# Layer 0 attention in a deeper pipeline, the read-out first, with one extra fp32 product in front of each three transposes

## The chip, the cores and the metric

The program runs on 1 core of one Trainium2 chip. The metric is the device time of one execution in microseconds (us), lower is better. A core has five engines that run side by side and wait for each other by semaphores: TensorE (PE: products and transposes, results into PSUM), VectorE (DVE), ScalarE (ACT), GpSimd (POOL) and SyncE (SP, which issues DMAs here).

## The reference, cut to what matters

The whole network is one layer of neighbourhood attention on 4 images of 56x56 pixels (layer 0), one layer of full attention over 3136 tokens, and a routed feed-forward layer. The change touches only layer 0's attention: each pixel looks at a 7x7 window, with 8 heads, a low rank of 4 for queries and keys, and values of 32 numbers.

```python
attn = jnp.einsum('bhijc,bhikjlc->bhijkl', q, k_win)
attn = attn + bias.transpose(0, 1, 3, 2, 4)[None]
attn = jax.nn.softmax(attn.reshape(B, nh, H, W, K * K), axis=-1)
attn = attn.reshape(B, nh, H, W, K, K)
out = jnp.einsum('bhijkl,bhikjld->bhijd', attn, v_win)
```

## The kernel before, in words

`layer0_attend` handles 8 iterations (`it`: 2 groups of 4 heads, times 4 images). Each iteration has 28 blocks (`n`: 4 row blocks by 7 column blocks) of 112 pixels, so there are 224 blocks. For each block and each of 4 heads (`hh`; `m = 4 n + hh` counts the heads' tiles) the work is:

1. PE `scores` (L452): 112 queries against 280 keys, four products side by side, one PSUM bank a head.
2. DVE `maxima` (L509): add the bias (which masks what is outside a window), write `sm`, keep the row's extreme in `mx`.
3. ACT `exponentials` (L559): exponential into the tile `P`, with the row's sum in `rs`.
4. DVE `normalise` (L516, L519): reciprocals for a pair of heads, then two multiplications of `P`.
5. PE `turn` (L462): three transposes of `P` into one of three PSUM banks.
6. ACT `copy_turned` (L567): that bank into `PTs`.
7. PE `mix` (L474): 12 products of `PTs` with the values into the single bank OUT. An fp32 product is recorded as two instructions, a transpose or an fp32r product as one, so the trace counts 24 here.
8. DVE `read_out` (L527): bank OUT into `yT`, from where SP stores it.

POOL's `place` (L425 and L428) rearranges the next iteration's queries and keys, a pair of casts for each of four pieces; the piece `rb` waits until 28 (rb + 1) tiles of the present iteration are scored. SP loads values (L359) a row block ahead and the next queries and keys (L350, L352).

The order of the work is written out by hand, engine by engine. Before, PE does scores of block n, turns block n-1 and mixes block n-2. DVE does the maxima of n, normalises the first pair of n, reads out n-2, normalises the second pair. ACT does four exponentials of n, then four copies of n. Each engine runs iterations in hardware loops (`Fori`) whose body is one iteration of 28 blocks.

Of the kernel before, what the change touches and what calls it, by code (L numbers as in the profile page):

```python
# [281 lines left out]
def layer0_attend(nc, A, S):  # L282
# [6 lines left out]
    with ExitStack() as ctx:  # L289
# [22 lines left out]
        P = sb("P", [TT, 8, KEYS])  # L312
# [13 lines left out]
        steps = sem("steps")  # L326

        def since(eng, semaphore, it, each, k):

            if not isinstance(it, int) or it * each + k > 0:  # L330
                eng.wait_ge(semaphore, it * each + k)
# [12 lines left out]
        def _(sp):  # L344
# [23 lines left out]
            def store(g, b, it, rb):  # L368
                sp.wait_ge(out_read, it * NBLK + 7 * (rb + 1))
                sp.sem_inc(steps, 1)  # L370
                since(sp, stored, it, 4 * 16, 16 * rb)
                if not isinstance(it, int):
                    sp.sem_inc(steps, 1)
# [3 lines left out]
            def body(g, b, before, after, switch=False, switched=False):  # L377
                it = g * B + b
                for rb in range(ROW_BLOCKS):
                    since(sp, mixed, it, NBLK, 7 * rb)  # L380
                    if not isinstance(it, int):
                        sp.sem_inc(steps, 1)
                    if rb < ROW_BLOCKS - 1:
                        load_values(g, b, rb + 1)
                    elif after is not None:
                        load_values(after[0], after[1], 0)
                    if rb > 0:
                        store(g, b, it, rb - 1)
                    elif before is not None:
                        store(*before, it - 1, ROW_BLOCKS - 1)  # L390
                    if rb == 0 and after is not None:
                        sp.wait_ge(placed, it * 8 + 8)
                        if not isinstance(it, int):
                            sp.sem_inc(steps, 1)
                        load_qk(*after)
                    if switch and rb == 1:
                        load_bias(1, 0)
                    if switch and rb == 3:
                        load_bias(1, 1)
                    if switched and rb == 0:  # L400
                        load_bias(1, 2)
# [8 lines left out]
            body(0, 0, None, (0, 1))  # L410
            with sp.Fori(1, B - 1) as b:
                body(0, b, (0, b - 1), (0, b + 1))
            body(0, B - 1, (0, B - 2), (1, 0), switch=True)
            body(1, 0, (0, B - 1), (1, 1), switched=True)
            with sp.Fori(1, B - 1) as b:
                body(1, b, (1, b - 1), (1, b + 1))
            body(1, B - 1, (1, B - 2), None)
# [4 lines left out]
        def _(pool):  # L422
# [13 lines left out]
            with pool.Fori(1, ITS) as it:  # L436
                pool.wait_ge(loaded, (it + 1) * NLOAD)
                for rb in range(ROW_BLOCKS):
                    pool.wait_ge(scored, it * U - U + 28 * (rb + 1))
                    pool.sem_inc(steps, 1)  # L440
                    place(it, rb)

        @block.tensor
        def _(pe):
# [11 lines left out]
            def turn(it, n):  # L456
                for hh in range(4):
                    m = 4 * n + hh
                    pe.wait_ge(normed, it * U + m + 1)
                    since(pe, copied, it, U, bank_free_at(m) + 1)  # L460
                    for c, k0 in enumerate(CHUNK_FROM):
                        last = pe.transpose(PS[0:CHUNK, turn_bank(m), TT * c:TT * c + TT], P[:, m % 8, k0:k0 + CHUNK],  # L462
                                            idn[:, :])
                    last.then_inc(turned, 1)
# [13 lines left out]
            def body(it, first):  # L478
                for n in range(NBLK):
                    scores(it, n)  # L480
                    if n >= 1:
                        turn(it, n - 1)
                    elif not first:
                        turn(it - 1, NBLK - 1)
                    if n >= 2:
                        mix(it, n - 2)
                    elif not first:
                        mix(it - 1, NBLK - 2 + n)
# [3 lines left out]
            body(0, True)  # L492
            with pe.Fori(1, ITS) as it:
                body(it, False)
# [5 lines left out]
        def _(dve):  # L500
            def maxima(it, n):
                rb, tc = divmod(n, COL_BLOCKS)
                case = 3 * ROW_CASE[rb] + COL_CASE[tc]
                for hh in range(4):
# [3 lines left out]
                    dve.sem_inc(steps, 1)  # L508
# [4 lines left out]
            def normalise(it, n, pair):  # L513
# [4 lines left out]
                for k in (m, m + 1):  # L518
                    dve.tensor_scalar(P[:, k % 8, :], P[:, k % 8, :], rc[:, k % 8:k % 8 + 1], None, ALU.mult)\  # L519
                       .then_inc(normed, 1)  # L520
# [9 lines left out]
            def body(it, first, fresh):  # L530
                for n in range(NBLK):
                    if fresh and n in (0, 7, 21):
                        dve.wait_ge(bias_loaded[(0, 7, 21).index(n)], (it // B + 1) * 64)
                    maxima(it, n)
                    normalise(it, n, 0)
                    if n >= 2:
                        read_out(it, n - 2)
                    elif not first:
                        read_out(it - 1, NBLK - 2 + n)
                    normalise(it, n, 1)  # L540

            dve.memset(vt[0:14, :, :, 2, :], 0.0).then_inc(zeroed, 1)
            body(0, True, True)
            with dve.Fori(1, B) as it:
                body(it, False, False)
            body(B, False, True)
            with dve.Fori(B + 1, ITS) as it:
                body(it, False, False)
            read_out(ITS - 1, NBLK - 2)
            read_out(ITS - 1, NBLK - 1)  # L550

        @block.scalar
        def _(act):
            def exponentials(it, n):
                for hh in range(4):
                    m = 4 * n + hh
                    act.wait_ge(maxed, it * U + m + 1)
                    since(act, turned, it, U, m - 7)
                    act.activation(P[:, m % 8, :], sm[:, hh, :], ACT.Exp, bias=mx[:, m % 8:m % 8 + 1], scale=-1.0,  # L559
                                   accum_out=rs[:, m % 8:m % 8 + 1]).then_inc(exped, 1)  # L560

            def copy_turned(it, n):
                since(act, mixed, it, NBLK, n - 1)
                for hh in range(4):
                    m = 4 * n + hh
                    act.wait_ge(turned, it * U + m + 1)
                    act.activation(PTs[:, m % 8, :], PS[0:CHUNK, turn_bank(m), 0:3 * TT], ACT.Copy).then_inc(copied, 1)  # L567

            def body(it):
# [4 lines left out]
            body(0)  # L574
            with act.Fori(1, ITS) as it:
                body(it)
# [1585 lines left out]
```

## Time and profile before

| what | us |
|---|---|
| median of 3 runs (lowest to highest) | 8198.59 (8192.75 to 8208.01) |
| profiled execution | 8213.32 |
| its span in the trace | 8211.5 |
| layer 0 attention in it, first score product to last read-out | 1107.9, from 489.4 to 1597.3 |

The profile cuts the span into 40 slices of 205 us. Layer 0 attention is the slices from the third to the eighth. "PEclk" is the clock that TensorE was granted, as a share of 2.4 GHz; 0.50 is 1.2 GHz. In timelines a row is a run of like instructions: start, time until the last one's end, engine, line, operation, tiles, count, and in brackets how long the engine had been idle and what released it. Durations of PE are modelled; the distance from start to start is the better measure, and in one row it is (the row's time minus one instruction's own) over (count - 1).

### The profile page before, as it was taken

The page shows a single profiled execution, that of the slowest core. Times are in us where ns is not written, and L with a number is a line of the kernel's source. Part 1 is how long each engine was busy: PE and PEld are TensorE (multiplying, and loading weights), DVE is VectorE, ACT ScalarE, POOL GpSimd, SP SyncE. Part 2 cuts the span into 40 slices and gives each one's busy share as a digit, 9 for nine tenths or more (in the row PEclk, how much of TensorE's full clock was granted, in tenths as well). Part 3 has the DMA queues.
Part 4 walks back from the last instruction along what each step waited for, and adds up shares of the span by engine and source line. Part 5 has one row for each costly group of instructions (what it writes and reads, how often), then busy time and mean ns, then how long its engine had stood idle before and what let it go on. Part 6 is the DMA issues. An engine that isn't in the chain of part 4 may idle for free. (4 is left out here: it accounts for less than half of the span.)

```text
span 8211.5 us, 152999 instructions
## 1 busy us (share of the span) xinstructions
PE 7229.3 (88%) x45616; PEld 4362.4 (53%) x45616; DVE 5407.6 (66%) x12877; ACT 4102.7 (50%) x9367; POOL 3716.6 (45%) x2395
## 2 busy tenths in 40 slices
PE   4558878798999999999999999999999988809999
PEld 3336555565545545545545555455455333708888
DVE  3347777665987767767767777677677201718888
ACT  0047777622005656555656655556565665104444
POOL 4010001011006666666666656566666666355554
PEclk8755565699559999999999999999999999859999
DMA  5432221277100121121121211201210101711221
GB/s 161 133 104 59 61 65 50 73 253 232 39 13 22 37 55 33 27 58 35 32 61 26 50 43 30 64 22 38 55 38 25 40 4 38 224 29 56 58 57 32
DMA packets 403203, 520.46 MB, mean 63 GB/s; under 512 B 64096, under 2 KB 355474, under 8 KB 399063
## 3 DMA queue, kind: packets, MB, share of 16 engines
q1 hardware_dynamic: 379687, 469.02, 21.2%
q0 software_dynamic: 22640, 40.75, 1.8%
q8 instruction: 429, 7.03, 0.4%
q14 instruction: 447, 3.66, 0.2%
HBM read 339.07 MB, written 200.10 MB: 66 GB/s over the span
## 5 line engine op out<-in xcount | busy, mean ns | idle before, releaser
L1253 DVE TENSOR_REDUCE a_tops<-a_ps 128x1 f32<-128x448 f32 (+1 forms) x5600 | 3074.4, 616 | 1089.0 <-PE a_ps L1155 1071.2
L1376 POOL TENSOR_TENSOR a_added<-a_P 128x896 f32<-128x896 f32 x1344 | 2801.6, 2105 | 2091.9 <-ACT a_P L1353 2091.9
L1353 ACT ACTIVATE a_P<-a_ps 128x448 f32<-128x448 f32 (+1 forms) x5600 | 2657.6, 547 | 2119.0 <-PE a_ps L1224 2087.8
L1224 PE MATMUL a_ps<-a_qp,a_kp 98*128 98x448 f32 (+1 forms) x5600 | 2157.0, 400 | 97.8 <-ACT a_P L1353 72.7
L1155 PE MATMUL a_ps<-a_hk,a_hq 96*128 96x448 f32 (+1 forms) x4900 | 1818.8, 381 | 1.8 <-DMA a_hq<-scratch_q 1.7
L1224 PEld LDWEIGHTS a_ps<-a_qp,a_kp 98*128 98x128 f32 (+1 forms) x5600 | 1031.0, 188 | 1291.4 <-ACT a_P L1353 737.3
L1175 PE MATMUL a_ps<-a_P,a_vt 128*32 128x448 f32 (+1 forms) x11200 | 1336.2, 549 | 0.0
L1155 PEld LDWEIGHTS a_ps<-a_hk,a_hq 96*128 96x128 f32 (+1 forms) x4900 | 916.7, 187 | 263.3 <-DVE a_tops L1253 170.7
L462 PE MATMUL n_ps<-n_idn,n_P 112*98 112x112 f32 x2688 | 517.3, 365 | 194.2 <-DVE n_P L519 177.8
L1191 PE MATMUL a_ps<-a_added,a_ones 128*32 128x448 f32 x5376 | 649.2, 555 | 0.0
L1175 PEld LDWEIGHTS a_ps<-a_P,a_vt 128*32 128x32 f32 (+1 forms) x11200 | 290.1, 109 | 514.1 <-issue 387.9
L462 PEld LDWEIGHTS n_ps<-n_idn,n_P 112*98 112x98 f32 x2688 | 406.1, 180 | 293.3 <-DVE n_P L519 271.6
L567 ACT ACTIVATE n_PTs<-n_ps 98x336 f32<-98x336 f32 x896 | 393.5, 451 | 239.3 <-PE n_ps L462 198.0
L1276 DVE RECIPROCAL a_sums<-a_sums 128x112 f32<-128x112 f32 x224 | 185.4, 836 | 488.8 <-ACT a_sums L1328 488.8
L559 ACT ACTIVATE n_P<-n_sm,n_mx 112x280 f32<-112x280 f32 x896 | 459.5, 518 | 61.4 <-DVE n_mx L509 46.9
L425 POOL CAST n_qp<-n_qn 128x784 fp32r<-128x784 f32 x32 | 52.9, 1655 | 907.6 <-PE n_ps L452 527.4
L1143 PE MATMUL a_ps<-a_kp,a_qp 96*128 96x448 f32 (+1 forms) x700 | 370.2, 726 | 22.5 <-DMA a_kp<-scratch_k 22.5
L509 DVE CUSTOM_DVE_ANT_0 n_sm<-n_ps,n_bias 112x280 f32<-112x280 f32 x896 | 348.3, 445 | 63.4 <-PE n_ps L452 48.1
L519 DVE TENSOR_SCALAR n_P<-n_P,n_rc 112x280 f32<-112x280 f32 x896 | 350.4, 433 | 15.7
L1956 ACT ACTIVATE e_h<-e_ps,e_b 128x512 f32<-128x512 f32 (+1 forms) x256 | 172.1, 672 | 351.4 <-PE e_ps L1916 326.3
L1929 PE MATMUL e_ps<-e_w2h,e_hTh 128*128 128x256 f32 (+1 forms) x1024 | 299.0, 292 | 36.8 <-DVE e_widest L2038 36.8
L1143 PEld LDWEIGHTS a_ps<-a_kp,a_qp 96*128 96x128 f32 (+1 forms) x700 | 198.4, 284 | 194.3 <-DVE a_tops L1253 169.1
(193 smaller groups left out, 7533.6 us busy)
## 6 DMA issues: line engine op xcount, KB each, us to landing
a_qp<-scratch_q SPq DMA_DIRECT2D x168, 224.0 KB, 3.9
a_kp<-scratch_k SPq DMA_DIRECT2D x96, 320.0 KB, 5.4
a_hk<-scratch_k SPq DMA_DIRECT2D x84, 336.0 KB, 5.0
scratch_t<-o_ts SPq DMA_DIRECT2D x56, 448.0 KB, 5.7
scratch_vw<-scratch_v SPq DMA_DIRECT2D x56, 392.0 KB
n_vt<-scratch_vw SPq DMA_DIRECT2D x64, 343.0 KB
a_hq<-scratch_q SPq DMA_DIRECT2D x84, 200.0 KB, 3.2
e_w<-in_w SPq DMA_DIRECT2D x16, 1024.0 KB, 7.0
```

The source lines that it names most:

```text
L462: last = pe.transpose(PS[0:CHUNK, turn_bank(m), TT * c:TT * c + TT], P[:, m % 8, k0:k0 + CHUNK], idn[:, :])
L519: dve.tensor_scalar(P[:, k % 8, :], P[:, k % 8, :], rc[:, k % 8:k % 8 + 1], None, ALU.mult)\
L559: act.activation(P[:, m % 8, :], sm[:, hh, :], ACT.Exp, bias=mx[:, m % 8:m % 8 + 1], scale=-1.0, accum_out=rs[:, m % 8:m % 8 + 1]).then_in ...
L567: act.activation(PTs[:, m % 8, :], PS[0:CHUNK, turn_bank(m), 0:3 * TT], ACT.Copy).then_inc(copied, 1)
L1143: pe.matmul(PS[0:rows_of(t), i % FIRST_BANKS, 0:GW], qp[0:96, hh, 128 * t:128 * t + rows_of(t)], kp[0:96, hh, GW * k:GW * k + GW], start=T ...
L1155: pe.matmul(PS[0:rows_of(t), MAX + i % MAXES, 0:GW], hq[:, 128 * t:128 * t + rows_of(t)], hk[:, GW * k:GW * k + GW], start=True, stop=True ...
L1175: last = pe.matmul(PS[HD * hh:HD * hh + HD, MIX, 0:GW], vt[0:rows, t, HD * hh:HD * hh + HD], P[0:rows, (2 * n + hh // 2) % (2 * RING), hh ...
L1191: last = pe.matmul(PS[HD * hh:HD * hh + HD, SUM, 0:GW], ones[:, :], added2[:, (2 * (PAIRS * j + u) + hh // 2) % 6, hh % 2, :], start=(u == ...
L1224: pe.matmul(PS[0:rows_of(t), i_s % 3, 0:GW], kp[0:98, hh, 128 * t:128 * t + rows_of(t)], qp[0:98, hh, GW * j:GW * j + GW], start=True, sto ...
L1253: dve.tensor_reduce(tops[0:rows_of(t), KT * hh + t, k:k + 1], PS[0:rows_of(t), bank, 0:GW], AX_X, ALU.max).then_inc(topped, 1)
L1353: act.activation(P[0:rows_of(t), (2 * n + pair) % (2 * RING), hh % 2, :], PS[0:rows_of(t), (4 * n + hh) % 3, 0:GW], ACT.Exp).then_inc(expe ...
L1376: pool.tensor_tensor(added2[:, a % 6, :, :], P[:, (2 * n + pair) % (2 * RING), :, :], P[:, (2 * n + 2 + pair) % (2 * RING), :, :], ALU.add ...
```

## The change

All of it is in `layer0_attend`.

- Deep order. PE does scores of n, turns n-2 (was n-1), mixes n-3 (was n-2). DVE reads out n-4 first (was n-2, in the middle), then does the maxima of n, then normalises both pairs of n-1 (was n). ACT alternates one exponential of n with one copy of n-2 (was four and four, copies of n). `P` has 16 slots for it (`RP`, was 8).
- One extra product. In front of the three transposes of each head, PE multiplies the 112x112 unit matrix with itself in fp32 into columns 384 to 495 of the bank that the transposes write. Nothing reads it. It waits for the bank to be free; the wait for `normed` now stands behind it.
- The hardware loops are gone: all eight iterations are written out on every engine, and the waits are on constants.

```diff
-        P = sb("P", [TT, 8, KEYS])
+        RP = 16
+        P = sb("P", [TT, RP, KEYS])
...
             def turn(it, n):
                 for hh in range(4):
                     m = 4 * n + hh
+                    since(pe, copied, it, U, bank_free_at(m) + 1)
+                    pe.matmul(PS[0:TT, turn_bank(m), 384:384 + TT], idn[:, :], idn[:, :], start=True, stop=True)
                     pe.wait_ge(normed, it * U + m + 1)
-                    since(pe, copied, it, U, bank_free_at(m) + 1)
...
                     scores(it, n)
-                    if n >= 1:
-                        turn(it, n - 1)
+                    if n >= 2:
+                        turn(it, n - 2)
                     elif not first:
-                        turn(it - 1, NBLK - 1)
-                    if n >= 2:
-                        mix(it, n - 2)
+                        turn(it - 1, NBLK - 2 + n)
+                    if n >= 3:
+                        mix(it, n - 3)
...
-            body(0, True)
-            with pe.Fori(1, ITS) as it:
-                body(it, False)
+            for it in range(ITS):
+                body(it, it == 0)
...
+                    if n >= 4:
+                        read_out(it, n - 4)
+                    elif not first:
+                        read_out(it - 1, NBLK - 4 + n)
                     maxima(it, n)
-                    normalise(it, n, 0)
-                    if n >= 2:
-                        read_out(it, n - 2)
+                    if n >= 1:
+                        normalise(it, n - 1, 0)
...
+            def body(it, first):
                 for n in range(NBLK):
-                    exponentials(it, n)
-                    copy_turned(it, n)
+                    for hh in range(4):
+                        exponential(it, 4 * n + hh)
+                        if n >= 2:
+                            copy_turned(it, 4 * n - 8 + hh)
```

PE within a steady block, before: the last transposes of a block, its `mix`, the next scores, the next transposes (L462 transposes, L474 mix, L452 scores; `waits` names the semaphores).

```order
L462 MATMUL n_ps<-n_idn,n_P 98x112 [waits n0_copied,n0_normed]
L462 MATMUL n_ps<-n_idn,n_P 98x112 x2
L474 MATMUL n_ps<-n_PTs,n_vt 32x112 [waits n0_out_read,n0_copied]
L474 MATMUL n_ps<-n_PTs,n_vt 32x112 x11
L452 MATMUL n_ps<-n_kp,n_qp 112x280 [waits n0_maxed]
L452 MATMUL n_ps<-n_kp,n_qp 112x280 x3
L462 MATMUL n_ps<-n_idn,n_P 98x112 [waits n0_copied,n0_normed]
L462 MATMUL n_ps<-n_idn,n_P 98x112 x2
```

PE at the same place now (L448 the extra product, L451 transposes, L463 mix, L440 scores).

```order
L448 MATMUL n_ps<-n_idn 112x112 [waits n0_copied]
L451 MATMUL n_ps<-n_idn,n_P 98x112 [waits n0_normed]
L451 MATMUL n_ps<-n_idn,n_P 98x112 x2
L463 MATMUL n_ps<-n_PTs,n_vt 32x112 [waits n0_out_read,n0_copied]
L463 MATMUL n_ps<-n_PTs,n_vt 32x112 x11
L440 MATMUL n_ps<-n_kp,n_qp 112x280 [waits n0_maxed]
L440 MATMUL n_ps<-n_kp,n_qp 112x280 x3
L448 MATMUL n_ps<-n_idn 112x112 [waits n0_copied]
```

A product that waits for the copies alone now stands in front of each group of transposes, and the groups behind the scores are those of two blocks ago.

ACT before, around one block's end (L559 exponential, L567 copy; the register instructions belong to the loop).

```order
L559 ACTIVATE n_P,n_rs<-n_sm,n_mx 112x280 [waits n0_turned,n0_maxed]
L331 REGISTER_ALU
L567 ACTIVATE n_PTs<-n_ps 98x336 [waits n0_turned,n0_mixed]
L567 ACTIVATE n_PTs<-n_ps 98x336 [waits n0_turned] x3
L557 REGISTER_ALU
```

ACT now (L550 exponential, L557 copy).

```order
L557 ACTIVATE n_PTs<-n_ps 98x336 [waits n0_turned]
L550 ACTIVATE n_P,n_rs<-n_sm,n_mx 112x280 [waits n0_turned,n0_maxed]
L557 ACTIVATE n_PTs<-n_ps 98x336 [waits n0_turned,n0_mixed]
L550 ACTIVATE n_P,n_rs<-n_sm,n_mx 112x280 [waits n0_turned,n0_maxed]
L557 ACTIVATE n_PTs<-n_ps 98x336 [waits n0_turned]
```

Exponentials and copies alternate, and no register instruction stands between them.

## Rows read from the trace of the kernel before

**Rows 1.** The page: the span, and the granted clock in 40 slices.

```profile
span 8211.5 us, 152999 instructions
PEclk8755565699559999999999999999999999859999
```

**Rows 2.** Windows view, whole layer 0 attention.

```profile
core 0: us, PE busy (x) PEld busy (x) DVE busy (x) ACT busy (x) POOL busy (x), PEclk, DMA share, GB/s
489.40:1597.30 1107.90, 888.47 (x8960) 658.78 (x8960) 795.71 (x3360) 850.81 (x2688) 94.67 (x58) 0.60 0.23 58
```

**Rows 3.** Waits in that stage: waiter, releaser, total us, times, longest.

```profile
DVE n_rc L516 <- ACT n_P L559: 275.3, 224, 6.9
ACT n_PTs L567 <- PE n_ps L462: 198.0, 328, 5.2
```

**Rows 4.** Timeline of a block at granted clock 0.50.

```profile
1401.99 1.35 PE L474 MATMUL n_ps<-n_PTs,n_vt 98*32 98x112 f32 x24
1403.27 0.58 PE L452 MATMUL n_ps<-n_kp,n_qp 16*112 16x280 f32 x4
1404.22 2.48 PE L462 MATMUL n_ps<-n_idn,n_P 112*98 112x112 f32 x12 [0.38 <-DVE n_P L519]
1407.90 0.58 PE L452 MATMUL n_ps<-n_kp,n_qp 16*112 16x280 f32 x4
```

**Rows 5.** Timeline, PE in a block at granted clock 1.00.

```profile
1202.48 0.43 PE L452 MATMUL n_ps<-n_kp,n_qp 16*112 16x280 f32 x4
1203.43 0.78 PE L462 MATMUL n_ps<-n_idn,n_P 112*98 112x112 f32 x6 [0.52 <-DVE n_P L519]
...
1205.16 0.78 PE L474 MATMUL n_ps<-n_PTs,n_vt 98*32 98x112 f32 x24
...
1206.20 0.40 PE L452 MATMUL n_ps<-n_kp,n_qp 16*112 16x280 f32 x4 [0.26 <-DVE n_mx L509]
```

**Rows 6.** Timeline, DVE and ACT in the same stretch.

```profile
1204.95 0.45 DVE L509 CUSTOM_DVE_ANT_0 n_sm<-n_ps,n_bias 112x280 f32<-112x280 f32 x1
1204.98 0.79 ACT L567 ACTIVATE n_PTs<-n_ps 98x336 f32<-98x336 f32 x2 [0.16 <-PE n_ps L462]
...
1205.32 0.45 DVE L509 CUSTOM_DVE_ANT_0 n_sm<-n_ps,n_bias 112x280 f32<-112x280 f32 x1
...
1206.68 0.52 ACT L559 ACTIVATE n_P<-n_sm,n_mx 112x280 f32<-112x280 f32 x1
1206.82 0.17 DVE L516 RECIPROCAL n_rc<-n_rs 112x2 f32<-112x2 f32 x1 [0.67 <-ACT n_P L559]
...
1207.19 0.52 ACT L559 ACTIVATE n_P<-n_sm,n_mx 112x280 f32<-112x280 f32 x1
...
1208.59 0.45 DVE L509 CUSTOM_DVE_ANT_0 n_sm<-n_ps,n_bias 112x280 f32<-112x280 f32 x1
```

**Rows 7.** The page's groups: ACT's copies.

```profile
L567 ACT ACTIVATE n_PTs<-n_ps 98x336 f32<-98x336 f32 x896 | 393.5, 451 | 239.3 <-PE n_ps L462 198.0
```

**Rows 8.** Timeline at a turn of the hardware loop.

```profile
1184.00 0.58 PE L452 MATMUL n_ps<-n_kp,n_qp 16*112 16x280 f32 x4 [2.65 <-issue]
...
1187.07 2.29 PE L462 MATMUL n_ps<-n_idn,n_P 112*98 112x112 f32 x11 [2.14 <-issue]
...
1192.37 0.53 ACT L559 ACTIVATE n_P<-n_sm,n_mx 112x280 f32<-112x280 f32 x1 [2.52 <-issue]
```

**Rows 9.** Timeline at a pair of POOL's casts.

```profile
1248.32 1.77 POOL L425 CAST n_qp<-n_qn 128x784 fp32r<-128x784 f32 x1 [8.93 <-PE n_ps L452]
...
1249.03 2.85 DVE L519 TENSOR_SCALAR n_P<-n_P,n_rc 112x280 f32<-112x280 f32 x2
...
1250.05 1.67 POOL L428 CAST n_kp<-n_kn 128x784 fp32r<-128x784 f32 x1
```

**Rows 10.** Windows view: three of layer 0 attention, one of layer 1, one of the feed-forward.

```profile
1523.40:1557.60 34.20, 31.59 (x312) 24.09 (x309) 24.11 (x113) 28.60 (x89) 0.00 (x0) 0.50 0.17 43
1202.60:1209.40 6.80, 4.71 (x66) 3.24 (x70) 5.78 (x27) 6.01 (x22) 0.00 (x0) 1.00 0.50 109
1209.40:1219.70 10.30, 9.33 (x104) 7.11 (x96) 7.29 (x36) 8.71 (x29) 0.00 (x0) 0.50 0.28 51
...
2040.00:2450.00 410.00, 381.96 (x737) 203.55 (x741) 373.86 (x705) 6.99 (x15) 11.89 (x4) 0.50 0.15 33
7610.00:7670.00 60.00, 57.68 (x373) 52.16 (x372) 53.99 (x148) 28.44 (x49) 34.47 (x42) 1.00 0.11 33
```

More of the change, by code:

```diff
@@ L325, in layer0_attend @@
         mixed, out_read, stored = sem("mixed"), sem("out_read"), sem("stored")
-        steps = sem("steps")
         def since(eng, semaphore, it, each, k):
-            if not isinstance(it, int) or it * each + k > 0:
+            if it * each + k > 0:
                 eng.wait_ge(semaphore, it * each + k)
@@ L435, in _ @@
                 place(0, rb)
-            with pool.Fori(1, ITS) as it:
+            for it in range(1, ITS):
                 pool.wait_ge(loaded, (it + 1) * NLOAD)
@@ L540, in body @@
-                    normalise(it, n, 1)
-            dve.memset(vt[0:14, :, :, 2, :], 0.0).then_inc(zeroed, 1)
[L543 to L550, printed above, removed]
+                        normalise(it - 1, NBLK - 1, 0)
+                    if n >= 1:
+                        normalise(it, n - 1, 1)
+                    elif not first:
+                        normalise(it - 1, NBLK - 1, 1)
@@ L552, in _ @@
+            dve.memset(vt[0:14, :, :, 2, :], 0.0).then_inc(zeroed, 1)
+            for it in range(ITS):
+                body(it, it == 0, it % B == 0)
+            for pair in range(2):
+                normalise(ITS - 1, NBLK - 1, pair)
+            for n in range(NBLK - 4, NBLK):
+                read_out(ITS - 1, n)
         @block.scalar
         def _(act):
[L554 to L560, printed above, removed]
@@ L575, in _, with exponential, copy_turned @@
-            with act.Fori(1, ITS) as it:
-                body(it)
+            def exponential(it, m):
+                act.wait_ge(maxed, it * U + m + 1)
+                since(act, turned, it, U, m - RP + 1)
+                act.activation(P[:, m % RP, :], sm[:, m % 4, :], ACT.Exp, bias=mx[:, m % 8:m % 8 + 1], scale=-1.0,
+                               accum_out=rs[:, m % 8:m % 8 + 1]).then_inc(exped, 1)
+            def copy_turned(it, m):
+                if m % 4 == 0:
+                    since(act, mixed, it, NBLK, m // 4 - 1)
+                act.wait_ge(turned, it * U + m + 1)
+                act.activation(PTs[:, m % 8, :], PS[0:CHUNK, turn_bank(m), 0:3 * TT], ACT.Copy).then_inc(copied, 1)
@@ new lines, in body @@
+            def body(it, first):
+                for n in range(NBLK):
+                    for hh in range(4):
+                        exponential(it, 4 * n + hh)
+                        if n >= 2:
+                            copy_turned(it, 4 * n - 8 + hh)
+                        elif not first:
+                            copy_turned(it - 1, U + 4 * n - 8 + hh)
+            for it in range(ITS):
+                body(it, it == 0)
+            for m in range(U - 8, U):
+                copy_turned(ITS - 1, m)
```

48 lines of the change are left out of this document (14 added, 34 removed).

## The prediction

> **What bounds the kernel now.** I read first the page's row of the granted clock [rows 1]: in layer 0 attention it stands near half, while the slices of the later layers are mostly at 9. The windows view of the stage [rows 2] gives its size, 1107.9 us for 224 blocks or 4.95 us a block, and a mean clock of 0.60: with only the levels 0.50 and 1.00, a fifth of the time at 2.4 GHz, four fifths at 1.2. No engine is full: PE is busy 888 us of 1108, ACT 851, DVE 796.
>
> The waits [rows 3] show a ring: DVE waits 275 us for exponentials and ACT 198 us for transposes, each in every block. The timeline shows how it closes. At 1.2 GHz a block repeats after 1407.90 - 1403.27 = 4.63 us [rows 4]; at 2.4 GHz after 1206.20 - 1202.48 = 3.72 us [rows 5]. PE's pace sets the block although PE waits in it, because an exponential, its normalisation, its transposes and its copy follow one another with only one block of distance. On top come the turns of the loop, where engines stand in "issue" for 2 to 3 us, PE twice and ACT once [rows 8], and POOL's cast pairs, during which two multiplications of DVE take 2.85 us in place of 0.64 [rows 9].
>
> **The change part by part.**
>
> *The ring goes.* Every consumer now takes what was made a block earlier. What is late next is the sum of work of an engine, so I add these up per block.
> ACT: exponentials start 1207.19 - 1206.68 = 0.51 apart; two copies in a row take 0.79, one is 0.45 [rows 6, 7], so they start 0.34 apart. 4 x 0.51 + 4 x 0.34 = 3.40 us.
> DVE: a maximum every 1205.32 - 1204.95 = 0.37; from the first reciprocal to the next block's first maximum, which holds both normalisations and the read-out, 1208.59 - 1206.82 = 1.77 [rows 6]. 4 x 0.37 + 1.77 = 3.25 us.
> PE at 2.4 GHz: 12 transposes at (0.78 - 0.27)/5 = 0.10, 24 mix instructions about 0.70, scores about 0.25, the turnover to mix 0.1 [rows 5] (0.27, one transpose's own time, is my estimate): 2.25 us.
>
> *The extra products.* One fp32 product is two instructions. They are not in the trace; the nearest row is the transpose with the same 112 columns, 0.10 at 2.4 GHz and (2.48 - 0.39)/11 = 0.19 at 1.2 [rows 4, 5] (0.39 an estimate likewise). 8 a block: 0.8 or 1.5 us. Bounds: 0 (they run while PE waits for `normed`) to twice that, were both the load and the stream of each exposed. I take once. Nothing waits for them but PE's own queue: the transposes behind them, then copies. PE at 2.4 GHz: 3.05 us, below ACT's 3.40. PE at 1.2 GHz: mix up to the next scores 1403.27 - 1401.99 = 1.28, transposes 12 x 0.19 = 2.28, products 1.52, scores about 0.35, turnover 0.13: 5.56 us. So at the low clock PE alone would bound a block, at 5.55 us, 0.9 more than now; at the high one ACT does, and the products are free.
>
> *Which clock.* Before, PE rises to 2.4 GHz after dense stretches at 1.2 and falls again when, at 2.4, it starts to wait: 6.8 us with PE busy 4.71 at 1.00, then 10.3 us with 9.33 at 0.50 [rows 10]. After the change PE at 1.2 GHz never waits, denser than any stretch of this stage before. At 2.4 GHz it works 3.05 of 3.5 us; before it worked 2.25 of 3.72. The feed-forward holds 1.00 over 60 us with PE busy 57.7 [rows 10]. I take it that 2.4 GHz mostly holds, and is lost where PE has to stand still.
>
> *The fast block.* Floor 3.40 (ACT), ceiling 3.72, what the old order reaches at 2.4 GHz. One chain comes close to the floor: read-out 0.27, maximum 0.45, exponential 0.51, copy 0.45, product and transposes 0.6, mix 0.78, with some 0.3 of signals 3.3 to 3.4 us, because bank OUT is single. Two engines and this chain are within 0.15 us; jitter adds up. I take 3.6: 224 x 3.6 = 806 us.
>
> *POOL's casts.* 28 pairs fall into the running stage. Each now held DVE for 2.85 - 0.64 = 2.2 us [rows 9]. DVE has nearly no spare time to catch up; the bounds are 0.5 (slack in `P` and `sm`) and 3.4 (the pair's full length, as all four multiplications now stand in a row). I take 2.0: 56 us.
> By the Trainium skill (SBUF — State Buffer, section on who interferes with whom) VectorE in a two-port mode and GpSimd take a shared port pair by an exclusive lock, and the loser blocks for the whole instruction. The trace agrees: the two multiplications end with the second cast. By that rule alone, which leaves no slack, the term would be the full pairs, 28 x 3.4 = 95 us.
>
> *Clock lost behind these.* If each pair drops the clock for as long as a fast stretch lasts now, 6.8 us, at 5.55 in place of 3.6 per block, it costs 6.8 x (1 - 3.6/5.55) = 2.4 us; 28 x 2.4 = 67 us. Bounds 0 and, for 10.3 us each, 101.
>
> *The loops.* The three waits at a turn, one after the other on the ring, are 2.65 + 2.14 + 2.52 = 7.3 us [rows 8], 7 times: 51 us, which are in the 1108 and not in the new sum. Straight code is new for seven of eight iterations; its fetching costs nothing where no branch is taken [rows 4], bounds 0 and the same 51. Fill and drain of the deeper order: 15 us.
> SP's queries and keys for the next iteration (32 DMAs) need some 35 us of an iteration that is now about 105 long, and values a row block of 25: hidden. The loss if not would be single microseconds per iteration.
>
> *Sum.* 806 + 56 + 67 + 15 = 944 us against 1108: 164 us less. 8213 - 164 = 8049 for an execution like the profiled one; this was 14.7 us above the median of the runs, so 8034, I say 8035. With all terms low (3.45 a block, 28 x 1, 28 x 0.7, 15): 836, 272 less, 7927. With all high (3.72, 95, 101, 20): 1049, 59 less, 8140; with the fetching's 51 as well 8190.
>
> **The rivals.**
>
> *B: the clock goes on swinging.* For it: before, every fast stretch of this stage fell, and PE still has pauses at 2.4 GHz. Against it: PE's waits shrink from 1.5 us to 0.5 a block. With as much time low as high, 6.8 us each: 1.23 + 1.89 blocks in 13.6 us, 4.36 a block, 977 + 56 + 15 = 1048, 60 less, 8139. With 10.3 low to 6.8 high as in [rows 10]: 4.57 a block, 1094, 14 less, 8184, which is no change.
>
> *C, the other side: the clock never rises.* Mechanism: the extra products lengthen PE's block at 1.2 GHz to 5.56 us, PE is the bound, and DVE and ACT have 2 us spare, in which the casts hide. 224 x 5.55 + 15 = 1258: 150 more, 8348. The end at which it costs begins where 3.6 + 1.95 x + 0.25 for the casts reaches (1108 - 15)/224 = 4.88, that is with more than x = 0.53 of the blocks low. For it: 34 us of this stage at PE busy 31.6 stayed at 0.50, and layer 1 has 410 us with 382 busy at 0.50 [rows 10]. Against it: that busy time is modelled and contains waits; the real starts of this stage, with 0.4 and 0.6 us of pause a block, often sufficed to rise.
> The Trainium skill (TensorE: Matmul & The Clock Gate, Part 4) says that transposes do not count as PE-busy in the way products do. If so the products are what counts, and half of PE's time does not: that speaks for C. The trace speaks against: the clock rose in this stage with transposes as its largest part.
>
> *D: a wait of the new order that I don't see* keeps the block at the old pace: nothing but the loops is won or lost, within 16 us of before.
>
> **How the numbers follow.** My forecast 0.54, B 0.31, C 0.10, D 0.05. About 16 us (0.2%) is what a measurement tells from no change. Faster: 0.54 + 0.31 less a tenth of B that ends at no change (0.03) = 0.82, and a third of D, 0.02, gives 0.84. Same: 0.03 + 0.02 = 0.05. Slower: C and the rest of D, 0.11. The range: from all terms low, 7930, up into B, 8165, which leaves out C and the slow end of B. The forecast's own range is 7930 to 8140, the fetching's bound aside, which I hold for unlikely.
>
> **What would show it.** Right: the stage's mean clock above 0.85; starts of ACT's exponentials 0.85 to 0.9 apart, alternating with copies, in 3.45 to 3.7 us a block; ACT busy over 85% of the stage; no "issue" waits of 2 us at iteration ends; DVE's multiplications still stretched at POOL's casts, and a low stretch behind them. Wrong: clock between 0.6 and 0.8 and blocks of two kinds, 3.6 and 5.5 (B); clock 0.50 and 5.5 throughout (C); a block over 3.9 at 2.4 GHz would mean that the chain through bank OUT is longer than I added up.

## The result, and the profile after

The changed kernel takes 7928.72 us (median of four runs, 7921.81 to 7931.02). The kernel before, run beside it, takes 8202.67 us (four runs, 8192.75 to 8208.01). The ratio is 0.9666, its 95% interval 0.9649 to 0.9683. That is 274 us less where 164 were forecast, and the median lies 1 us below the range, whose low end was 7930 (two of the four runs lie inside). The profiled execution took 7931.02 us, against 8213 before.

The page after, beside [rows 1]:

```profile
span 7929.2 us, 152182 instructions
PEclk8779999995599999999999999999999999859999
```

The 5s of layer 0 attention are gone and the stage is about one slice of 200 us shorter. The windows view of the stage, beside [rows 2]:

```profile
490.10:1331.20 841.10, 795.70 (x10752) 634.66 (x10752) 767.28 (x3360) 772.95 (x2688) 93.83 (x58) 0.96 0.29 75
```

The stage went from 1107.9 to 841.1 us, 267 less, which is the change. The other 15 us between the two spans lie behind the stage (6614 us before, 6598 after), in a part that no edit touches and that takes between 6592 and 6623 us in the profiles of the runs below. PE has 1792 more instructions and is still busy for less time, since the granted clock went from 0.60 to 0.96. ACT is now busy 92% of the stage and DVE 91%. Per block the stage takes 3.75 us in place of 4.95.

The waits of the stage after, beside [rows 3] (waiter, releaser, total us, times, longest):

```profile
ACT n_P L550 <- DVE n_mx L498: 108.3, 46, 46.1
PEld n_ps L448 <- ACT n_PTs L557: 98.9, 346, 2.9
...
PE n_ps L451 <- DVE n_P L508: 10.2, 15, 2.6
ACT n_PTs L557 <- PE n_ps L451: 2.0, 4, 1.0
```

Both halves of the old ring are gone. DVE's 275 us for exponentials don't appear, and ACT's 198 us for transposes are 2.0. PE now waits most for free banks, that is for ACT's copies. (46 us of ACT's first row lie ahead of the first block.)

The page's group of the copies after, beside [rows 7]:

```profile
L557 ACT ACTIVATE n_PTs<-n_ps 98x336 f32<-98x336 f32 x896 | 391.1, 437 | 2.6 <-PE n_ps L451 2.0
```

The copies cost ACT what they cost before. What vanished is the idle time in front of them, 239 us before and 2.6 now.

A steady block, timeline, beside [rows 5] and [rows 6]:

```profile
1262.10 0.40 PE L440 MATMUL n_ps<-n_kp,n_qp 16*112 16x280 f32 x4
1262.24 0.27 DVE L516 COPY n_yT<-n_ps 128x112 f32<-128x112 f32 x1
1262.26 0.52 ACT L550 ACTIVATE n_P<-n_sm,n_mx 112x280 f32<-112x280 f32 x1
1262.43 0.45 PE L448 MATMUL n_ps<-n_idn 112*112 112x112 f32 x2
1262.64 0.45 DVE L498 CUSTOM_DVE_ANT_0 n_sm<-n_ps,n_bias 112x280 f32<-112x280 f32 x1
...
1262.77 0.44 ACT L557 ACTIVATE n_PTs<-n_ps 98x336 f32<-98x336 f32 x1
1263.13 0.53 ACT L550 ACTIVATE n_P<-n_sm,n_mx 112x280 f32<-112x280 f32 x1
...
1264.80 0.78 PE L463 MATMUL n_ps<-n_PTs,n_vt 98*32 98x112 f32 x24
1265.52 0.40 PE L440 MATMUL n_ps<-n_kp,n_qp 16*112 16x280 f32 x4
```

The block repeats after 1265.52 - 1262.10 = 3.42 us. Of the 223 distances between two blocks' scores, 202 lie wholly at full clock; their median is 3.417, and 182 of all lie within 0.05 of it. Exponentials and copies alternate on ACT without a gap: 1262.26, 1262.77, 1263.13. PE's longest wait in this block is 0.23 us, for a copy.

The rest is at POOL's casts. In six of seven iterations the first pair (due after 7 scored blocks) comes late: it waits for its DMA until about the 14th block, where the second pair is due too, and both run back to back (once 1 us apart). Timeline there:

```profile
643.04 1.64 POOL L414 CAST n_qp<-n_qn 128x784 fp32r<-128x784 f32 x1 [50.06 <-DMA n_kn<-scratch_qk]
643.23 2.94 DVE L508 TENSOR_SCALAR n_P<-n_P,n_rc 112x280 f32<-112x280 f32 x2
...
644.61 1.39 POOL L417 CAST n_kp<-n_kn 128x616 fp32r<-128x616 f32 x1
...
645.94 1.67 POOL L414 CAST n_qp<-n_qn 128x784 fp32r<-128x784 f32 x1
...
646.27 3.12 DVE L508 TENSOR_SCALAR n_P<-n_P,n_rc 112x280 f32<-112x280 f32 x2
...
647.56 1.67 POOL L417 CAST n_kp<-n_kn 128x784 fp32r<-128x784 f32 x1
...
649.97 0.53 ACT L550 ACTIVATE n_P<-n_sm,n_mx 112x280 f32<-112x280 f32 x1 [4.44 <-DVE n_mx L498]
```

Four casts in a row hold DVE's multiplications for 2.94 and 3.12 us, ACT starves for 4.44 us, and PE with it. The windows of that stretch, of the one behind it, and of the next:

```profile
643.00:650.00 7.00, 3.87 (x49) 2.77 (x48) 6.93 (x12) 2.56 (x10) 6.19 (x4) 1.00 0.28 88
650.40:657.20 6.80, 6.22 (x50) 5.35 (x51) 5.30 (x25) 5.55 (x21) 0.00 (x0) 0.50 0.00 0
657.40:672.00 14.60, 14.59 (x220) 11.48 (x218) 12.72 (x60) 13.65 (x49) 0.00 (x0) 1.00 0.38 98
```

PE works 3.87 of 7.00 us, the clock falls to 1.2 GHz for 6.8 us, and is back at 2.4 behind that. There are ten such low stretches behind the fill, 61 us in all: five behind two pairs in a row, four behind the fourth pair, one behind the first pair of the first iteration, which comes alone. The third pair (21st block) costs a block 0.8 us and leaves the clock as it is. The fourth, due at the last block's scores, costs more:

```profile
1012.40 2.25 POOL L417 CAST n_kp<-n_kn 128x1120 fp32r<-128x1120 f32 x1
1012.49 2.60 DVE L508 TENSOR_SCALAR n_P<-n_P,n_rc 112x280 f32<-112x280 f32 x2
```

Its second cast is the longest, 2.25 us, and the first block of the next iteration takes 5.1 to 6.2 us. By the distances between blocks, seven iterations lose 40 us around the first two pairs (35 of them where these run in a row), 6 at the third and 18 at the fourth, the slow blocks at the low clock included.

### The profile page after: what moved, and what is told of

Read it like the earlier page. It is cut to its first block and busy times, and to the rows that moved or that the text cites. A ratio compares the mean times of both kernels' runs of the same rounds, so it can differ in the third digit from the quotient of the medians.

```text
span 7929.2 us, 152182 instructions
## 1 busy us (share of the span) xinstructions
PE 7120.8 (90%) x47408; PEld 4323.5 (55%) x47408; DVE 5376.1 (68%) x12877; ACT 4022.7 (51%) x9367; POOL 3714.0 (47%) x2395
## 5 line engine op out<-in xcount | busy, mean ns | idle before, releaser
L550 ACT ACTIVATE n_P<-n_sm,n_mx 112x280 f32<-112x280 f32 x896 | 467.9, 522 | 108.4 <-DVE n_mx L498 108.3
L451 PE MATMUL n_ps<-n_idn,n_P 112*98 112x112 f32 x2688 | 421.2, 267 | 10.2 <-DVE n_P L508 10.2
L448 PE MATMUL n_ps<-n_idn 112*112 112x112 f32 x1792 | 373.1, 291 | 30.7 <-ACT n_PTs L557 29.8
L557 ACT ACTIVATE n_PTs<-n_ps 98x336 f32<-98x336 f32 x896 | 391.1, 437 | 2.6 <-PE n_ps L451 2.0
L508 DVE TENSOR_SCALAR n_P<-n_P,n_rc 112x280 f32<-112x280 f32 x896 | 334.2, 415 | 16.0
L448 PEld LDWEIGHTS n_ps<-n_idn 112*112 112x112 f32 x1792 | 255.4, 183 | 112.5 <-ACT n_PTs L557 98.9
```

What stands on the lines that cost most here:

```text
L448: pe.matmul(PS[0:TT, turn_bank(m), 384:384 + TT], idn[:, :], idn[:, :], start=True, stop=True)
L550: act.activation(P[:, m % RP, :], sm[:, m % 4, :], ACT.Exp, bias=mx[:, m % 8:m % 8 + 1], scale=-1.0, accum_out=rs[:, m % 8:m % 8 + 1]).the ...
```

## The experiments

Ratios are to the kernel before, run on the same chip beside them. "Full-clock block" is the median distance of two blocks' scores where the granted clock is 1.00. Columns of the windows rows are those of [rows 2]. Two repetitions of the changed kernel went along as a yardstick; other runs are compared with it through their ratios.

> The changed kernel itself, on the chip of the following runs, as their yardstick: ratio to the kernel before 0.966 to 0.968.

> The changed kernel as the yardstick of this chip: ratio 0.965 to 0.967.

They took 7926.25 us (ratio 0.9654, interval 0.9636 to 0.9673) and 7929.18 (0.966, 0.9641 to 0.9679). A window around the stage of the first is below (it begins 1 us early; the stage itself takes 829.2 us); that of the second takes 839.7 us at a clock of 0.96:

```profile
496.50:1326.50 830.00, 786.33 (x10752) 626.36 (x10752) 764.76 (x3360) 771.68 (x2688) 93.92 (x58) 0.97 0.29 77
```

So the stage of one and the same kernel differs by 12 us between profiles, with the block at 3.42 in both; less than that is not read from one profile below.

### The loops alone

```diff
-            with pe.Fori(1, ITS) as it:
+            for it in range(1, ITS):
```
(the same in the bodies of the other engines; all else as before)

> The kernel before with its hardware loops written out and nothing else changed. Theory of the prediction: 7 turns at 7.3 us go, 51 us, program about 8150. Rival (straight code is fetched more slowly, or the waits at the turn were hidden): 0 to 20 us, program 8180 to 8203.

8173.38 us, ratio 0.9934 (0.9918 to 0.9951): 54 us less by the ratio, 52 by the medians.

```profile
494.20:1556.60 1062.40, 882.97 (x8960) 654.51 (x8960) 793.08 (x3360) 848.00 (x2688) 94.59 (x58) 0.60 0.23 59
```

The stage gives 45 us. The clock stays at 0.60. The term of 51 us from [rows 8] was right to within these figures, and the straight code brought no stall of its own that can be seen.

### The product: taken out, put into the old order, replaced, doubled

Taken out of the changed kernel:

```diff
-                    pe.matmul(PS[0:TT, turn_bank(m), 384:384 + TT], idn[:, :], idn[:, :], start=True, stop=True)
```

> The changed kernel without the extra product; the deep order and the straight code stay. Theory 1 (the product is what holds TensorE at 2.4 GHz): at 2.4 GHz PE works 2.25 of 3.42 us a block and the clock falls again and again, to a mean of 0.6 to 0.7 in layer 0 attention; a block takes about 4.05 us at 1.2 GHz (5.56 less the product's 1.52) and 3.42 at 2.4; about 3.8 on average, stage some 920 us, program about 8010. Theory 2 (the order does it all, the product is a passenger): clock or no clock, a block stays at 3.42, program within 10 us of 7929.

7976.41 us, ratio 0.970 (0.9684 to 0.9717).

```profile
494.70:1358.90 864.20, 727.49 (x8960) 510.87 (x8960) 765.39 (x3360) 771.96 (x2688) 92.61 (x58) 0.80 0.29 73
```

This lies between the two theories, which had 8010 and 7929. Nearly the whole gain is there without the product. 132 blocks run at full clock, with a median of 3.39 us; behind casts the clock stays low for 7 to 48 us, with blocks of 4.23 us, in place of 3 to 10 us with the product. The product raises the clock from 0.80 to 0.96, but a low block without it costs only 4.23 us, since PE then has 1.5 us less to do at 1.2 GHz. It is worth 0.4%, some 23 to 35 us of the stage.

Put into the kernel before:

```diff
-                    pe.wait_ge(normed, it * U + m + 1)
                     since(pe, copied, it, U, bank_free_at(m) + 1)
+                    pe.matmul(PS[0:TT, turn_bank(m), 384:384 + TT], idn[:, :], idn[:, :], start=True, stop=True)
+                    pe.wait_ge(normed, it * U + m + 1)
```

> The kernel before (old order, hardware loops) with the extra product alone. Theory 1: the product keeps the clock high here too, a block is near the 3.72 us of the old ring at 2.4 GHz, or up to 0.2 more as the product stands in the ring; 224 x 3.85 + 51 for the loops + 56 for the casts = 970 us in the stage, program about 8065. Rival: in the old ring PE waits for the others, the clock still falls, and the product lengthens each block at 1.2 GHz by what does not fit into PE's 0.7 us of waiting; about 5.2 us a block, program 8250 to 8350.

8216.36 us, ratio 0.9988 (0.9978 to 0.9999).

```profile
493.20:1613.50 1120.30, 913.60 (x10752) 732.79 (x10752) 798.53 (x3360) 857.63 (x2688) 93.05 (x58) 0.84 0.22 57
```

The time is neither that of the theory (8065) nor of the rival (8250 to 8350). The clock goes from 0.60 to 0.84 and the time stays. On the old ring the products lie on the path: the full-clock block is 4.16 us (3.79 before, the median of 17), the low one 5.79 (4.64). A higher granted clock by itself was no gain here.

Two unread transposes in its place:

```diff
-                    pe.matmul(PS[0:TT, turn_bank(m), 384:384 + TT], idn[:, :], idn[:, :], start=True, stop=True)
+                    for _ in range(2):
+                        pe.transpose(PS[0:TT, turn_bank(m), 384:384 + TT], idn[:, :], idn[:, :])
```

> The changed kernel with two unread transposes of the unit matrix in place of each extra product: as many instructions on as many columns. If transposes keep the clock as products do, the clock in the stage stays at 0.95 and the program within 10 us of 7929. If transposes do not count as products do, the clock falls as in the kernel without the product, and the time is that kernel's.

7948.41 us, ratio 0.966 (0.9644 to 0.9676).

```profile
495.40:1331.90 836.50, 771.79 (x10752) 610.22 (x10752) 764.90 (x3360) 768.21 (x2688) 93.77 (x58) 0.96 0.29 76
```

The same clock as with the product, and the stage within the spread of its profiles. Transposes hold the clock as products do here. The full-clock block is 3.39 us in place of 3.42; at head 3 the transposes behind start 0.25 us after the unread pair, and 0.28 us after the product. The rule that spoke for rival C (the Trainium skill, TensorE: Matmul & The Clock Gate, Part 4) would have this run at 0.80, like the one without; the measurement decides against it.

Doubled (the line a second time):

> The changed kernel with two extra products in a row in place of one. Theory 1 (an fp32 product costs TensorE 2 x 0.098 us at 2.4 GHz, and is free up to ScalarE's 3.42 us a block): TensorE's block becomes 3.1 + 0.78 = 3.85 us and is the bound, 224 x 0.45 = 100 us more than the changed kernel, less a few where casts now hide. Theory 2 (the products run in TensorE's waiting time whatever their number): no change.

8003.6 us, ratio 0.975 (0.9731 to 0.9768), 77 us above the changed kernel run beside it, where 100 less a few were expected. Windows of the stage and PE's timeline in a block:

```profile
497.40:1406.20 908.80, 894.90 (x12544) 782.66 (x12544) 768.28 (x3360) 785.97 (x2688) 92.90 (x58) 0.99 0.27 70
```
```profile
1202.90 0.36 PE L449 MATMUL n_ps<-n_idn 112*112 112x112 f32 x2
1203.10 0.45 PE L452 MATMUL n_ps<-n_idn,n_P 112*98 112x112 f32 x3
```

PE is busy 98% of the stage and bounds it, at 3.95 us a block. One product takes 1203.10 - 1202.90 = 0.20 us, two instructions at 0.10, the price taken from the nearest row. The changed kernel's PE then needs about 3.95 - 0.8 = 3.15 us, close to the 3.05 of the sum.

Left out for the last head alone:

```diff
+                    if hh != 3:
                         pe.matmul(PS[0:TT, turn_bank(m), 384:384 + TT], idn[:, :], idn[:, :], start=True, stop=True)
```

> The changed kernel with the product in front of the transposes of heads 0 to 2 only. The block at 2.4 GHz is 3.42 us with all four products and 3.39 with none. If the chain through the single bank OUT (copy, product and transposes of head 3, mix, read-out, maximum, exponential) sets the 3.42, this product is the one in it and the block is 3.39 here; if it is ScalarE's work beside a busy TensorE, three products leave 3.41 and one gone changes nothing visible. The clock should hold as before: program within 10 us of the changed kernel, ratio 0.965.

7919.64 us, ratio 0.965 (0.9628 to 0.9672), not told apart from the changed kernel. The stage:

```profile
494.40:1323.80 829.40, 766.25 (x10304) 590.28 (x10304) 760.10 (x3360) 767.64 (x2688) 92.44 (x57) 0.94 0.29 76
```

The full-clock block is 3.390 us in place of 3.417. That fits the reading that the last head's product is in the chain through bank OUT, as the sum of that chain had it, and that beneath the chain ACT's own sum lies at 3.39.

### The order

Exponentials in a group, then copies:

```diff
                         exponential(it, 4 * n + hh)
+                    for hh in range(4):
                         if n >= 2:
```

> The changed kernel with ScalarE's work of a block grouped again: four exponentials of block n, then four copies of block n-2, in place of one and one. Theory 1 (a block is as long as ScalarE's own work, 3.42 us, whatever its order): no change, within 15 us of the changed kernel. Theory 2 (three banks of transposes and the two-block distance only suffice when copies are spread over the block): the transposes wait for banks, the block goes to 3.6 to 3.8 us, 40 to 85 us more.

8388.29 us, ratio 1.0227 (1.0206 to 1.0248): slower than before. The stage, and ACT's and DVE's timeline in it:

```profile
488.80:1780.30 1291.50, 1164.78 (x10752) 932.24 (x10752) 768.40 (x3360) 809.80 (x2688) 92.27 (x58) 0.64 0.19 49
```
```profile
1100.00 0.53 ACT L550 ACTIVATE n_P<-n_sm,n_mx 112x280 f32<-112x280 f32 x1 [1.93 <-DVE n_mx L498]
...
1102.06 1.10 ACT L557 ACTIVATE n_PTs<-n_ps 98x336 f32<-98x336 f32 x3
...
1103.37 0.78 PE L463 MATMUL n_ps<-n_PTs,n_vt 98*32 98x112 f32 x24
...
1104.22 0.28 DVE L516 COPY n_yT<-n_ps 128x112 f32<-128x112 f32 x1 [1.65 <-PE n_ps L463]
...
1104.62 0.45 DVE L498 CUSTOM_DVE_ANT_0 n_sm<-n_ps,n_bias 112x280 f32<-112x280 f32 x1
...
1105.11 0.53 ACT L550 ACTIVATE n_P<-n_sm,n_mx 112x280 f32<-112x280 f32 x1 [1.19 <-DVE n_mx L498]
```

The same instructions with the same depth, and 450 us more in the stage, where 85 was the most expected. The rows are the chain that the prediction added up, in order: exponential, copy, mix, read-out, maximum, exponential. The first copy now stands behind three more exponentials, 3 x 0.51 = 1.53 us, and the full-clock block is 4.95 us, which is 3.42 + 1.53. With PE waiting that long the clock swings, at 0.64.

Read-out behind the maxima and normalisations of its block:

```diff
-                    if n >= 4:
-                        read_out(it, n - 4)
...
                     maxima(it, n)
...
                         normalise(it - 1, NBLK - 1, 1)
+                    if n >= 4:
+                        read_out(it, n - 4)
```

> The changed kernel with the read-out of block n-4 behind the maxima and normalisations of its step in place of in front of them. Theory 1 (the chain read-out, maximum, exponential, copy, transposes, mix through the single bank OUT was close to the bound): with the read-out later the chain is broken in another place; mix n-3 waits for it, up to 1 us, and holds the next scores; block 3.7 to 4.2 us, 60 to 170 us more. Theory 2 (there is slack on either side): block 3.42 us, no change.

8201.96 us, ratio 0.9996 (0.9987 to 1.0006): nothing is left of the gain, where 60 to 170 us were expected to go. The stage, and waits between 520 and 1300 us:

```profile
493.50:1598.70 1105.20, 868.94 (x10752) 707.41 (x10752) 752.11 (x3360) 793.01 (x2688) 91.85 (x58) 0.89 0.22 57
```
```profile
DVE n_sm L498 <- PE n_ps L440: 238.5, 157, 2.5
...
PE n_ps L463 <- DVE n_yT L516: 164.5, 129, 3.4
```

PE's next mix waits for bank OUT, which is read only at the end of DVE's block; the scores queue behind that mix, and DVE waits for them. The full-clock block is 4.65 us, at a clock of 0.89. Depth, alternation on ACT and straight code together are worth nothing without the read-out first, and the run before shows that depth with the read-out first loses 2% without the alternation. Both have to be there.

### POOL's casts

Left out in iterations 1 to 7:

```diff
-                    place(it, rb)
+                    pool.sem_inc(placed, 2)
```

> The changed kernel with POOL's casts for iterations 1 to 7 left out (queries and keys of iteration 0 are used for all; what the stage computes is then not the reference's). Theory 1 (the casts block VectorE, and that also drops TensorE's clock): no low stretches after the start, 224 x 3.415 + 8 = 773 us in the stage, some 67 us less than the changed kernel. Theory 2 (the clock falls by itself from TensorE's pauses at 2.4 GHz): the low stretches stay, only the casts' direct stalls go, 25 to 45 us less.

7874.67 us, ratio 0.9599 (0.9579 to 0.9618), 52 us less than the changed kernel run beside it. The stage, and it without its fill:

```profile
490.80:1267.20 776.40, 765.19 (x10752) 608.74 (x10752) 722.39 (x3360) 767.85 (x2688) 2.09 (x1) 0.99 0.32 81
500.20:1268.00 767.80, 759.34 (x10720) 604.06 (x10720) 714.93 (x3324) 760.69 (x2663) 0.00 (x0) 1.00 0.31 79
```

No low stretch is left behind the fill. All that the casts cost, the lost clock included, is 52 us by the runs and 53 by the stages of the two profiles run beside each other (829 less 776), where 67 were expected. Against the first profile of the changed kernel (841) it is 65.

Casts waiting for other blocks, so that the pairs are apart:

```diff
-                    pool.wait_ge(scored, it * U - U + 28 * (rb + 1))
+                    pool.wait_ge(scored, it * U - U + 4 * (16, 19, 22, 28)[rb])
```

> The changed kernel with POOL's four pairs of casts of an iteration waiting for 16, 19, 22 and 28 scored blocks in place of 7, 14, 21 and 28. In the changed kernel the first pair waits for its data until about block 14 and runs right in front of the second, 6.4 us of casts in one piece, and nearly every low stretch of the clock lies behind that. Theory 1 (it is the length of the stall that drops the clock): most low stretches go, 20 to 40 us less than the changed kernel. Theory 2 (the stalls add up however they are spread): 0 to 8 us.

7915.41 us, ratio 0.9645 (0.9627 to 0.9664), 11 us less, which the intervals don't separate; 20 to 40, or 0 to 8, were expected. The stage takes 820.5 us.

Seven low stretches are left, each behind a pair: the two casts of one pair, 3.4 us without a break, can still cost the clock.

Every single cast waiting for its own block:

```diff
-                    pool.wait_ge(scored, it * U - U + 28 * (rb + 1))
-                    place(it, rb)
+                    pool.wait_ge(scored, it * U - U + 4 * (15, 18, 22, 28)[rb])
+                    place(it, rb, 0)
+                    pool.wait_ge(scored, it * U - U + 4 * (16, 19, 23, 29)[rb])
+                    place(it, rb, 1)
```
(`place` with part 0 casts the queries, with part 1 the keys)

> The changed kernel with each of POOL's eight casts of an iteration waiting for a block of its own (15, 16, 18, 19, 22, 23, 28, 29 scored blocks). If a single cast of 1.3 to 2.3 us fits into the slack of the four tiles of sm and the banks, about 0.8 us, the clock stays at 1.00 and each cast costs 0.3 to 0.9 us: 7 x 8 x 0.6 = 35 us of stalls in place of 68, 30 us less than the changed kernel. If the stalls only add up: no change, or up to 10 us more.

7872.75 us (7868.40 to 7873.97), ratio 0.9592 (0.9574 to 0.9609). The stage, it without its fill, and POOL and DVE at two casts:

```profile
493.50:1271.20 777.70, 765.28 (x10752) 608.80 (x10752) 724.36 (x3360) 768.53 (x2688) 94.11 (x58) 0.99 0.32 81
500.00:1271.00 771.00, 762.37 (x10736) 606.76 (x10734) 719.39 (x3338) 764.21 (x2672) 91.84 (x56) 1.00 0.31 80
```
```profile
1047.40 0.45 DVE L502 CUSTOM_DVE_ANT_0 n_sm<-n_ps,n_bias 112x280 f32<-112x280 f32 x1
...
1047.42 1.63 POOL L415 CAST n_qp<-n_qn 128x784 fp32r<-128x784 f32 x1 [8.61 <-PE n_ps L444]
...
1049.07 0.64 DVE L512 TENSOR_SCALAR n_P<-n_P,n_rc 112x280 f32<-112x280 f32 x2
...
1050.84 1.33 POOL L419 CAST n_kp<-n_kn 128x616 fp32r<-128x616 f32 x1 [1.78 <-PE n_ps L444]
```

POOL does the same work, 94 us of it, and it costs nothing that can be seen: the mean block is 3.438 us, against 3.432 without casts. A cast of 1.6 us that starts with a block's scores falls beside DVE's maxima, which it doesn't stretch, and the multiplications that follow take 0.64. This version beats both kernels: 4.1% below the one before, some 0.7% (over 50 us, where 30 were expected) below the changed one.

### Casts and product together

> The changed kernel without the extra product and without POOL's casts of iterations 1 to 7 (queries and keys of iteration 0 are used for all; what the stage computes is then not the reference's). Theory 1 (TensorE at 2.4 GHz with 2.3 of 3.4 us worked keeps its clock as long as nothing stalls; the product only shortens what follows a stall): clock 1.00 throughout and 3.39 us a block, 764 us in the stage, the time of the run without casts less 5. Theory 2 (the product is what holds the clock): low stretches without any stall, blocks of 4.23 us among those of 3.39, some 30 to 60 us more than the run without casts.

> The kernel with single casts, without the extra product. Theory 1 (the product holds the clock only across stalls, and spread casts hardly stall): within 10 us of the kernel with single casts and the product, ratio to before about 0.960, a few low stretches. Theory 2 (without the product each cast, however short, drops the clock): 30 us more, ratio about 0.964.

The edits are those above, two at a time. Without product and casts: 7885.35 us, ratio 0.9605 (0.9588 to 0.9623). Single casts without product: 7883.8 us, 0.9604 (0.9585 to 0.9624). The stage takes 788.7 us in the first; in the second:

```profile
493.40:1281.90 788.50, 649.74 (x8960) 441.51 (x8960) 719.40 (x3360) 763.25 (x2688) 93.68 (x58) 0.93 0.31 80
```

The second came out as its first theory said; the first lies between its two. PE keeps 2.4 GHz for 82 to 256 us at a time. One such stretch of the first run:

```profile
732.00:980.00 248.00, 199.62 (x2920) 132.46 (x2919) 233.66 (x1096) 247.70 (x877) 0.00 (x0) 1.00 0.36 90
```

Counted from start to start, as the prediction counted it, PE's work is some 2.3 us of a block of 3.39. Then the clock falls, in a pause of 1.0 us in the third block of an iteration, and stays low for 17 to 38 us at 4.23 us a block. The same pause in other iterations leaves it. With the product it doesn't fall there; with single casts that is worth 11 us of the stage (788.5 less 777.7), below what profiles or ratios tell apart.

## Why the prediction was right, and where it was wrong

**The mechanism was right, the amount was not.** 164 us less were forecast and 274 came, because three terms of the sum were too dear; the loops, the floor of 3.40 and the clock held. ACT's exponentials and copies alternate, 0.51 and 0.35 us from start to start; the clock is 0.96; ACT is busy 92%; the ring's waits are gone. From before to straight loops, to the new order without product, to the changed kernel, the stage goes 1107.9, 1062.4, 864.2, 841.1: 45 us for the loops, 198 for the order, 23 for the product. Forecast were only the sums: new blocks at 806 + 56 + 67 + 15 = 944, where 841 were measured, 103 too much. The remaining 7 of the 110 us between forecast and result lie outside the stage, within what that part differs by from profile to profile.

**The step "The fast block" was mis-sized: 3.6 us, measured 3.42.** The floor of 3.40 for ACT was right (3.39 without the last head's product), and so was the chain through OUT at 3.3 to 3.4; I then added 0.2 for jitter, since two engines and a chain lie within 0.15 us of each other. The exchange between them hardly jitters: 182 of 223 distances lie within 0.05 us of 3.42, and the others stand at casts, at the low clock, at the fill or at an iteration's third block. The 224 blocks are 765 us, not 806, 41 of the 103. DVE's 3.25 stands by its busy time of 722 us in 224 blocks without casts (3.22), and PE's 3.05 by the run with two products (3.15).

**The steps "POOL's casts" and "Clock lost behind these" were mis-sized: 56 + 67 = 123 us; 65 in the profile after, 53 in its repetition (841.1 and 829.2 less the 776 without casts), 52 by the runs without casts.** With 65 that is 58 of the 103. The parts are an estimate: 61 us at the low clock, with the forecast's 5.55 us a block, lose 61 x (1 - 3.42/5.55) = 24 us, and the rest, 41, are the casts' own. Three things were wrong. I let every one of 28 pairs drop the clock for 6.8 us; ten low stretches were measured. I took 2.0 us for a pair alone; the third pair costs 0.8, the fourth at least 1.7. That the slack in `P` and `sm`, my lower bound with 0.5, covers the rest of the third was not tried by itself. And the dearest casts, some 35 of the 65 us, are two pairs in a row, which I did not foresee: the wait for 28 scored tiles no longer sets when the first pair runs; the DMAs do. I had put the loads of queries and keys at 35 us of an iteration and called them hidden. From PE they are, but the first cast that waits for them starts 43 to 51 us into the iteration, when the first pair has been due since a quarter of its 105 us, and collides with the second. The Trainium skill (SBUF — State Buffer, section on who interferes with whom) gives an exclusive lock between such instructions, and the rows of 2.94 and 3.12 us agree with that for DVE. The 28 x 3.4 = 95 us that the prediction worked out from it as a price for the stage are not borne out, because a lock of one instruction isn't yet a loss of the block: the third pair's casts take some 3.3 us and cost 0.8.

**Fill and drain** are about 7 us, with 4 more for the third blocks below, not 15: the last 4.

**The loops** (51 us) were right: 52 to 54 by the runs of the straight loops, 45 by the stage.

**"Which clock" was right for a reason that was only half right.** I took it that 2.4 GHz is lost where PE has to stand still, and so it is. But I had weighed 2.25 us of work in 3.72 as what loses the clock before, and 3.05 in 3.5 as what holds it. The runs without product hold 1.00 for 82 to 256 us with PE at 2.3 of 3.39, without the extra work that I had counted on. Nor do the lengths of single pauses sort the cases. Before, it fell behind stretches whose longest pause was 0.84 us; with the read-out last it stood at 1.00 for 44 us with a pause of at least 1.16 us in every block:

```profile
573.50:617.50 44.00, 32.47 (x461) 25.46 (x462) 29.62 (x135) 31.96 (x110) 2.88 (x2) 1.00 0.19 50
```
```profile
582.70 0.78 PE L463 MATMUL n_ps<-n_PTs,n_vt 98*32 98x112 f32 x24 [1.16 <-DVE n_yT L516]
```

What these runs do show is that the product's part in the time is small.

**Rival B** (a swinging clock) is refuted by 0.96, yet it is what happens with ACT's instructions grouped (0.64). **Rival C** had the low block about right (5.79 us in the old order and with the read-out last, 5.70 with transposes, against 5.55), but the clock rises from it within a block or two, and with transposes as well as with products. **Rival D** was real too, only for another order: with the read-out last, depth brings nothing.

**Not settled:** why the clock without product falls in one pause of 1.0 us and not in others, and what of PE's work and pauses decides it. Why blocks at the third place of each iteration take 0.57 us more (they do without casts too) wasn't tried; that is 4 us in all.

## What to carry to other kernels

When a software pipeline gets deeper, write the block's order down as a chain from one single buffer back to itself; that chain and the busiest engine set the pace. Here they lay within 0.15 us of each other, and the larger of them, with nothing added, would have been the right figure. Ask of every helper engine what starts its work once the others are faster: work that was spread out by a counter can come in a heap when its DMA becomes the later one, and a wait of its own for each piece, placed beside instructions that it doesn't disturb, cost nothing here and gave 0.7%. Unread products that raise the granted clock are worth what the low blocks cost beyond the fast ones: here 0.4%, some 0.1% (which the runs don't tell from nothing) once the casts were spread, and nothing at all where they lay on the path.

## What the hardware showed that I had not expected

- An fp32 product of 112 columns is two instructions of 0.10 us at 2.4 GHz, the same as a transpose each, and its effect on the granted clock is that of two transposes (0.96 and 0.96, against 0.80 without).
- The clock held 1.00 for 768 us with PE busy 759 (no casts), for 248 us with PE busy 200 (no casts, no product), and for 44 us with PE busy 32 and pauses of 1.16 us (read-out last).
- A POOL cast beside DVE's maxima left them at 0.45 us; casts beside two multiplications stretched these from 0.64 to between 2.60 and 3.12 us.
- Eight iterations as straight code in place of hardware loops showed no cost in fetching, and saved 0.7%, seven turns of about 7 us.
